# Two attention layers rebuilt on units of two tiles, with heads in row groups and the scores formed twice

## The chip, the cores and the metric

The kernel runs on one core of a Trainium2 chip. The metric is the device time of one execution in microseconds (us). Engines are named as in the profile: PE is TensorE (PEld its weight loads), DVE is VectorE, ACT is ScalarE, POOL is GpSimd, SP is SyncE, which here only issues DMAs.

## What is computed

The input is 128 sequences of 64 tokens of width 128, and a context of the same shape. Four stages follow one another; everything is fp32.

```python
x = x + _L0_xattn_ref(_layernorm(x), ctx, ctx, ...)   # 16 heads of 8, gate, three layer norms
x = x + _L0_ffn_ref(_layernorm(x), ...)               # 128 -> 512 -> 512 -> 512 -> 128
x = x + _L1_xattn_ref(_layernorm(x), ctx, ctx, ...)   # 16 heads of 8
x = x + _L1_ffn_ref(_layernorm(x), ...)               # 128 -> 512 -> 128
# both attentions, per sequence and head:
scores = jnp.einsum('bqhd,bkhd->bhqk', q, k) * scale
attn = jax.nn.softmax(scores, axis=-1)
out = jnp.einsum('bhqk,bkhd->bqhd', attn, v)
# layer 0 only: out = layer_norm(sigmoid(qn @ Wg) * (out @ Wo + bo))
```

The softmax takes the maximum of each row away before the exp.

## The kernel before

A tile is two sequences, 128 rows by 128 features; there are 64. The prologue (`prepare`, L170) loads and turns the weights and loads all of x and of the context into `x_res` and `ctx_res`. `attention` (L374) is called for layer 0 (`gated`) and layer 1, and each call is followed by a feed-forward stage on chunks of four tiles. Each of the four is a block of its own, which begins when all engines have left the one before. The feed-forward stages are not touched.

In `attention` every engine runs the same steps j over the tiles (`Steps`, L42: lead 5, lag 9, a loop unrolled by 4 in the middle, straight code at both ends), and in a step it works on several tiles, each at another place of its pipeline. The order on an engine is the order of the code, and semaphores tie the engines. For one tile:

- DVE takes the statistics (L733, L757), POOL the power -1/2 (`rstd`, L663), ACT normalises (`normed`, L617), PE turns it (`ps_in`, L517), ACT copies it (`turned`, L572), PE makes q, k and v in `ps_qkv` (L550, L551, L554), ACT copies them (L597, L600, L605).
- POOL spreads k over the heads: `k_heads` (L647) is k, repeated 16 times and multiplied by a mask that leaves each copy the 8 rows of its head, 2048 columns. PE then forms all 16 heads' scores with the full depth of 128 rows (L492): four fp32 products of 512 columns in two column halves, into the two banks `ps_s`.
- DVE takes the maximum of each row (`top`, L750) and subtracts it (`prob`, L776). Since `ps_s` exists once, the scores of the next tile wait for `shifted`. ACT takes the exp (L624), PE turns the result in eight pieces (`ps_pt`, L543), ACT copies it (`prob_t`, L591), and PE multiplies by the values (L533), two heads at a time, in four column groups. Two extra columns of ones in `v_by_pair` give the denominators.
- ACT copies (`sums_t`, L584), PE turns (L509), DVE divides (L694, L703), PE turns (L524), ACT copies (`out_t`, L579), PE multiplies by Wo (L502), and DVE adds the result to x (layer 1, L690) or goes through bias, gate and layer norm (layer 0, L686 to L743, where L714 multiplies `rstd` by the gate).

An fp32 product is two instruction pairs in the records (weight load and matmul each twice); a transposition is one.

Of the kernel before, what the change touches and what calls it, by code (L numbers as in the profile page):

```python
# [18 lines left out]
P = 128  # L19
# [7 lines left out]
UNROLL = 4  # L27

# [13 lines left out]
class Steps:  # L42
# [3 lines left out]
    def __init__(self, total, lead, lag, unroll):  # L46
        self.total, self.first, self.last, self.unroll = total, -lead, total + lag, unroll
        self.lo = -(-lag // unroll) * unroll
        self.hi = (total - lead) // unroll * unroll
# [120 lines left out]
def prepare(nc, t, a):  # L170


    with ExitStack() as ctx:
# [13 lines left out]
        cols = sb("cols", [P, 10])  # L187
        rows = sb("rows", [P, 3, P])
# [11 lines left out]
        zeros_ready, ident_ready, consts_ready = sem("zeros_ready"), sem("ident_ready"), sem("consts_ready")  # L200
        v_zero_ready = sem("v_zero_ready")
# [7 lines left out]
        with nc.Block() as block:  # L209
            @block.sync  # L210
            def _(sp):
                xv = a["x"].rearrange("(t b) s d -> (b s) t d", b=PER_TILE)
                cv = a["ctx_1024"].rearrange("(t b) s d -> (b s) t d", b=PER_TILE)
                xs = t.x[:, :].rearrange("p (t d) -> p t d", d=P)
                cs = t.ctx[:, :].rearrange("p (t d) -> p t d", d=P)

                def load_tiles(n):
                    first, last = (t.load_steps + [t.tiles])[n:n + 2]
                    sp.dma_start(xs[:, first:last, :], xv[:, first:last, :]).then_inc(t.tiles_loaded[n], 16)
                    sp.dma_start(cs[:, first:last, :], cv[:, first:last, :]).then_inc(t.tiles_loaded[n], 16)  # L220
# [18 lines left out]
            def _(act):  # L239
                names = ["L0_xattn_bq", "L0_xattn_bk", "L0_xattn_bv", "L0_xattn_ln_q_g", "L0_xattn_ln_q_b",  # L240
                         "L0_xattn_ln_kv_g", "L0_xattn_ln_kv_b", "L1_xattn_b_q", "L1_xattn_b_k", "L1_xattn_b_v"]
                for n, k in enumerate(names):
                    act.dma_start(cols[:, n:n + 1], column(a[k])).then_inc(params_loaded, 16)
                act.dma_start(rows[:, 0, :], row_everywhere(a["L0_xattn_Wg"].rearrange("d a -> (d a)"))).then_inc(params_loaded, 16)
                act.dma_start(rows[:, 1, :], row_everywhere(a["L0_xattn_ln_q_b"])).then_inc(params_loaded, 16)
                act.dma_start(rows[:, 2, :], row_everywhere(a["L0_xattn_ln_q_g"])).then_inc(params_loaded, 16)
# [16 lines left out]
            def _(pool):  # L263
                nc.gpsimd.memset(t.ident[:, :], 0.0).then_inc(zeros_ready, 1)
                nc.gpsimd.memset(t.head_mask[:, :], 1.0).then_inc(zeros_ready, 1)
                nc.gpsimd.memset(t.minus_half[:, :], -0.5)
                pool.wait_ge(zeros_ready, 2)
# [3 lines left out]
                nc.gpsimd.affine_select(out=t.head_mask[:, :], in_=t.head_mask[:, :], compare_op=ALU.is_ge, fill=0.0,  # L271
                                        base=0, pattern=[[-HEAD_DIM, HEADS]], channel_multiplier=1).then_inc(consts_ready, 1)
                pool.wait_ge(consts_ready, 1)
                nc.gpsimd.affine_select(out=t.head_mask[:, :], in_=t.head_mask[:, :], compare_op=ALU.is_ge, fill=0.0,
                                        base=HEAD_DIM - 1, pattern=[[HEAD_DIM, HEADS]], channel_multiplier=-1).then_inc(consts_ready, 1)
# [1008 lines left out]
```

## Time and profile before

| | |
|---|---|
| median of 3 runs | 1400.15 us (1397.81 to 1401.39) |
| span of the profiled execution | 1397.6 us |
| PE busy | 1187.9 us, 85% |
| DVE busy | 1097.0 us, 78% |
| ACT busy | 1015.8 us, 73% |
| POOL busy | 650.3 us, 47% |
| HBM read, written | 12.80 MB, 4.19 MB |

The span runs from the first to the last instruction of one execution; the runs are timed from outside. The shares are means over five stretches with different limits: the prologue (to about 48 us), attention 0 (to about 559), feed-forward 0 (to about 920), attention 1 (to about 1284) and feed-forward 1. Busy time says how long an engine held instructions, and an instruction that is held up counts as busy. So the stretches have to be read one by one, and in them the waits and the order in time.

### The profile page before, as it was taken

The page shows a single profiled execution, that of the slowest core. Times are in us where ns is not written, and L with a number is a line of the kernel's source. Part 1 is how long each engine was busy: PE and PEld are TensorE (multiplying, and loading weights), DVE is VectorE, ACT ScalarE, POOL GpSimd, SP SyncE. Part 2 cuts the span into 40 slices and gives each one's busy share as a digit, 9 for nine tenths or more (in the row PEclk, how much of TensorE's full clock was granted, in tenths as well). Part 3 has the DMA queues.
Part 4 walks back from the last instruction along what each step waited for, and adds up shares of the span by engine and source line. Part 5 has one row for each costly group of instructions (what it writes and reads, how often), then busy time and mean ns, then how long its engine had stood idle before and what let it go on. Part 6 is the DMA issues. An engine that isn't in the chain of part 4 may idle for free. (4 is left out here: it accounts for less than half of the span.)

```text
span 1397.6 us, 33684 instructions
## 1 busy us (share of the span) xinstructions
PE 1187.9 (85%) x10683; PEld 840.6 (60%) x10683; DVE 1097.0 (78%) x2885; ACT 1015.8 (73%) x2107; POOL 650.3 (47%) x449
## 2 busy tenths in 40 slices
PE   2686767777777775799999999969999999998998
PEld 2454544444444453688888888746666666665886
DVE  3599999999999997567667666437777777777996
ACT  2576566666666664688888888758888888885896
POOL 2766656566565663000000000058888888884110
PEclk8799999999999997899999999989999999999999
DMA  9400000000000000000000000000000000000011
GB/s 243 125 2 1 1 0 0 0 0 0 0 0 0 0 2 2 1 1 0 0 0 0 0 0 0 1 0 2 2 0 0 0 0 0 0 2 2 27 42 53
DMA packets 22080, 17.81 MB, mean 13 GB/s; under 512 B 2369, under 2 KB 17601, under 8 KB 22017
## 3 DMA queue, kind: packets, MB, share of 16 engines
q1 hardware_dynamic: 19792, 16.52, 4.1%
q0 software_dynamic: 352, 0.27, 0.2%
q8 instruction: 36, 0.59, 0.2%
q10 hardware_dynamic: 1872, 0.20, 0.1%
q14 instruction: 28, 0.22, 0.1%
HBM read 12.80 MB, written 4.19 MB: 12 GB/s over the span
## 5 line engine op out<-in xcount | busy, mean ns | idle before, releaser
L647 POOL TENSOR_TENSOR k_heads<-k_t,head_mask 128x2048 f32<-128x2048 f32 x128 | 462.6, 3614 | 57.5 <-ACT k_t L597 57.5
L492 PE MATMUL ps_s<-k_heads,q_t 128*64 128x512 f32 x1024 | 266.4, 640 | 134.7 <-DVE prob L776 133.7
L750 DVE TENSOR_REDUCE top<-ps_s 128x16 f32<-128x1024 f32 x128 | 155.8, 1217 | 111.0 <-PE ps_s L492 110.9
L663 POOL TENSOR_TENSOR rstd<-spread,minus_half 128x1 f32<-128x1 f32 (+2 forms) x140 | 95.0, 678 | 285.1 <-DVE spread L770 198.4
L126 POOL TENSOR_TENSOR front_rstd<-front_spread,minus_half 128x4 f32<-128x4 f32 x32 | 33.4, 1045 | 375.3 <-DVE front_spread L119 375.3
L799 PE MATMUL g_ps<-g_h_lo,w_hi 128*128 128x512 f32 x512 | 206.7, 404 | 0.0
L1015 DVE TENSOR_TENSOR g_h_lo<-g_h,g_h_hi 128x512 fp32r<-128x512 f32 x192 | 132.5, 690 | 92.3 <-ACT g_h_hi L963 88.4
L492 PEld LDWEIGHTS ps_s<-k_heads,q_t 128*64 128x64 f32 x1024 | 74.1, 139 | 217.2 <-issue 208.3
L800 PE MATMUL g_ps<-g_h_hi,w_hi 128*128 128x512 f32 x512 | 202.5, 395 | 0.0
L714 DVE TENSOR_TENSOR y_scale<-rstd,gate 128x1 f32<-128x1 f32 x64 | 171.0, 2671 | 0.1
L591 ACT ACTIVATE prob_t<-ps_pt 128x1024 f32<-128x1024 f32 x128 | 131.0, 1024 | 50.1 <-PE ps_pt L543 50.0
L776 DVE TENSOR_TENSOR prob<-ps_s,top 128x1024 f32<-128x1024 f32 x128 | 155.1, 1212 | 0.3
L624 ACT ACTIVATE prob<-prob 128x1024 f32<-128x1024 f32 x128 | 134.1, 1047 | 14.4 <-DVE prob L776 14.3
L543 PE MATMUL ps_pt<-ident,prob 128*128 128x128 f32 x1024 | 139.8, 280 | 0.2 <-ACT prob L624 0.2
L572 ACT ACTIVATE turned<-ps_in 128x256 f32<-128x256 f32 x128 | 49.1, 383 | 119.8 <-PE ps_in L517 118.2
L963 ACT ACTIVATE g_h_hi<-g_h 128x512 fp32r<-128x512 f32 x192 | 121.3, 632 | 18.7 <-DVE g_h L1025 14.6
L543 PEld LDWEIGHTS ps_pt<-ident,prob 128*128 128x128 f32 x1024 | 109.7, 141 | 12.1 <-ACT prob L624 0.6
L502 PEld LDWEIGHTS ps_y<-wa,out_t 128*128 128x128 f32 x256 | 41.8, 205 | 116.5 <-issue 112.4
L799 PEld LDWEIGHTS g_ps<-g_h_lo,w_hi 128*128 128x128 f32 x512 | 97.2, 190 | 22.6
L800 PEld LDWEIGHTS g_ps<-g_h_hi,w_hi 128*128 128x128 f32 x512 | 97.2, 190 | 21.0
L955 ACT ACTIVATE g_h<-g_ps,s 128x512 f32<-128x512 f32 x128 | 87.3, 682 | 30.4 <-PE g_ps L800 24.6
L533 PE MATMUL ps_o<-prob_t,v_by_pair 128*32 128x64 f32 x4096 | 85.5, 225 | 0.7 <-ACT prob_t L591 0.6
(171 smaller groups left out, 2503.2 us busy)
## 6 DMA issues: line engine op xcount, KB each, us to landing
out_x<-x_res SPq DMA_DIRECT2D x16, 256.0 KB, 2.3
raw_mid<-in_L_ffn_h_w SPq DMA_DIRECT2D x2, 1024.0 KB, 13.9
x_res<-in_x SPq DMA_DIRECT2D x2, 512.0 KB, 8.0
ctx_res<-in_ctx SPq DMA_DIRECT2D x2, 512.0 KB, 9.3
raw_up<-in_L_ffn_w_w SPq DMA_DIRECT2D x2, 256.0 KB, 7.7
raw_w<-in_L_ffn_W SPq DMA_DIRECT2D x2, 256.0 KB, 5.8
raw_down<-in_L_ffn_w_w SPq DMA_DIRECT2D x1, 256.0 KB, 14.6
raw_l<-in_L_xattn_Wq SPq DMA_DIRECT2D x1, 64.0 KB, 2.1
```

The source lines that it names most:

```text
L492: last = nc.tensor.matmul(ps_s[b * SEQ:(b + 1) * SEQ, half * 512:(half + 1) * 512], q_t[:, u, b * SEQ:(b + 1) * SEQ], k_heads[:, u % 2, ha ...
L543: last = nc.tensor.transpose(ps_pt[:, hp * P:(hp + 1) * P], prob[:, s % 2, hp * P:(hp + 1) * P], t.ident[:, :])
L591: nc.scalar.activation(prob_t[:, s % 2, :, :], ps_pt[:, :].rearrange("p (n d) -> p n d", n=PAIRS), ACT.Copy).then_inc(prob_t_taken, 1)
L624: nc.scalar.activation(prob[:, u % 2, :], prob[:, u % 2, :], ACT.Exp).then_inc(exp_done, 1)
L647: nc.gpsimd.tensor_tensor(k_heads[:, s % 2, :, :], k_t[:, s, :].unsqueeze(1).to_broadcast([P, HEADS, P]), t.head_mask[:, :].unsqueeze(2).t ...
L714: nc.vector.tensor_tensor(y_scale[:, 0:1], rstd[:, slot_a, 2:3], gate[:, slot_a:slot_a + 1], ALU.mult)
L750: nc.vector.tensor_reduce(out=top[:, u % 2, :], in_=ps_s[:, :].rearrange("p (h k) -> p h k", h=HEADS), op=ALU.max, axis=AX.X).then_inc(top ...
L776: nc.vector.tensor_tensor(prob[:, u % 2, :].rearrange("p (h k) -> p h k", h=HEADS), ps_s[:, :].rearrange("p (h k) -> p h k", h=HEADS), top ...
L799: nc.tensor.matmul(out, w_hi, x_lo, start=first and w_lo is None, stop=False)
L800: return nc.tensor.matmul(out, w_hi, x_hi, start=False, stop=last)
L963: nc.scalar.activation(h_hi[level][:, o, :], h[:, o % 2, :], ACT.Copy).then_inc(hi_ready[level], 1)
L1015: nc.vector.tensor_tensor(h_lo[level][:, o, :], h[:, o % 2, :], h_hi[level][:, o, :].bitcast(F32), ALU.subtract).then_inc(lo_ready[level], 1)
```

## The change

Both attentions are rewritten; the feed-forward stages stay. The steps now run over 32 units of two tiles, with lead 4 and lag 5.

- Wq, Wk and their biases are permuted on the host, so that the 32 rows of a group g hold 8 features of each of four heads. After the projection (now 256 columns wide, L580, L581) ACT copies to `qk_t`, and eight DMAs on SP's queue (L885) lay the heads side by side: `qk` has head set m at columns m*256, in rows 32g to 32g+7. Row 32g+8 of q takes minus the row maximum, and the same row of k holds ones.
- The scores of a tile are 32 small products, 8 rows deep, 64 by 64, in four row groups that write alternately to the two column halves (L488). DVE takes the maximum (L762). PE turns the maxima of a unit (L606), ACT copies them with the sign turned, four DMAs (L894) put them into `qk`.
- Two steps later PE forms the scores again with the operands exchanged and nine rows deep (L499): they come out transposed and with the maximum taken away, in `ps_st`. ACT takes the exp straight from there into `prob_t`.
- So `k_heads`, the subtraction, the eight transpositions and the copy of `prob_t` are gone.
- The context no longer lies in SBUF: a DMA per unit brings it (L870), in layer 1 from a transposed copy laid out on the host, so that layer 1 doesn't turn it. In layer 0 POOL normalises it (L735).
- The gate's product is formed on PE (L594), and the gate's power and the output norm's power are one power on POOL (L742) of two columns per unit. POOL also makes the small operands of the norms (L713 to L731).

The core of the diff:

```diff
+UNIT_TILES = 2
+UNIT = UNIT_TILES * P
+GROUPS = 4
+SETS = HEADS // GROUPS
...
     T = t.tiles
-    steps = Steps(T, lead=5, lag=9, unroll=UNROLL)
+    N = T // UNIT_TILES
+    steps = Steps(N, lead=4, lag=5, unroll=UNROLL)
...
+        qk = sb("qk", [P, UNROLL, 2, SETS, UNIT])
...
+        ps_st = psum("ps_st", 2)
+        ps_av = psum("ps_av")
+        ps_mid = psum("ps_mid")
+        ps_turn = psum("ps_turn")
+        ps_vy = psum("ps_vy")
...
+                def scores(i, s, k):
+                    for m in range(SETS):
+                        for b in range(PER_TILE):
+                            at = slice(k * P + b * SEQ, k * P + (b + 1) * SEQ)
+                            for g in range(GROUPS):
+                                rows, h2, bank = slice(32 * g, 32 * g + HEAD_DIM), g % 2, g // 2
+                                col = bank * 512 + (m * PER_TILE + b) * SEQ
+                                last = nc.tensor.matmul(ps_s[h2 * SEQ:(h2 + 1) * SEQ, col:col + SEQ],
+                                                        qk[rows, s, 0, m, at], qk[rows, s, 1, m, at], start=True, stop=True)
+                    last.then_inc(scores_done, 1)
+
+                def shifted_scores(i, s, k):
+                    for m in range(SETS):
+                        for b in range(PER_TILE):
+                            at = slice(k * P + b * SEQ, k * P + (b + 1) * SEQ)
+                            for g in range(GROUPS):
+                                rows, h2, bank = slice(32 * g, 32 * g + HEAD_DIM + 1), g % 2, g // 2
+                                col = bank * 512 + (m * PER_TILE + b) * SEQ
+                                last = nc.tensor.matmul(ps_st[h2 * SEQ:(h2 + 1) * SEQ, col:col + SEQ],
+                                                        qk[rows, s, 1, m, at], qk[rows, s, 0, m, at], start=True, stop=True)
+                    last.then_inc(shifted_done, 1)
+
+                def weighted_values(i, s, k):
+                    for b in range(PER_TILE):
+                        for half in range(2):
+                            for c in range(4):
+                                hp = 4 * half + c
+                                last = nc.tensor.matmul(
+                                    ps_av[PAIR_COLS * c:PAIR_COLS * (c + 1), (2 * k + half) * P + b * SEQ:(2 * k + half) * P + (b + 1) * SEQ],
+                                    t.v_by_pair[:, s, (k * PER_TILE + b) * PAIRS + hp, :],
+                                    prob_t[:, k, hp % 2, hp // 2, b, :], start=True, stop=True)
+                    last.then_inc(pv_done, 1)
...
+                def exponential(i, k):
+                    wait(act, shifted_done, 2 * i + k + 1)
+                    wait(act, pv_done, 2 * i + k - 1)
+                    nc.scalar.activation(prob_t[:, k, :, :, :, :].rearrange("p h m b q -> p (h m b q)"), ps_st[:, :],
+                                         ACT.Exp).then_inc(exp_done, 1)
...
+                        for n in range(2):
+                            last = nc.scalar.activation(qk_t[:, s % 2, n, :], ps_mid[:, n * UNIT:(n + 1) * UNIT], ACT.Identity,
+                                                        bias=t.qk_bias[:, layer, n:n + 1])
+                        last.then_inc(qk_taken, 1)
...
+                        wait(act, top_turned, i + 1)
+                        before = (u - 2) % UNROLL
+                        wait(act, top_landed[before], landed(i - 2, before, 4))
+                        nc.scalar.activation(minus_top_t[:, s % 2, :], ps_turn[0:32, 0:P], ACT.Copy, scale=-1.0).then_inc(top_taken, 1)
...
+                        wait(pool, pool_chain, 2 * i + 1)
+                        nc.gpsimd.tensor_tensor(rstd[:, s, :, :], spread[:, s, :, :],
+                                                t.minus_half[:, 0:NORMS * UNIT_TILES].rearrange("p (n k) -> p n k", n=NORMS),
+                                                ALU.pow).then_inc(pool_chain, 1)
...
+                            last = nc.gpsimd.tensor_scalar(normed[:, s % 2, 1, k, :], ctx_in[:, s, k, :], rstd[:, s, 1, k:k + 1],
+                                                           offset[:, s, 1, k:k + 1], ALU.mult, ALU.add)
+                        last.then_inc(ctx_normed, 1)
...
+                def maximum(i, s, k):
+                    wait(dve, scores_done, 2 * i + k + 1)
+                    wait(dve, top_turned, i - 1)
+                    nc.vector.tensor_reduce(out=top[:, s % 2, :, k, :], in_=ps_s[:, :].rearrange("p (a b q) -> p a b q", b=PER_TILE, q=SEQ),
+                                            op=ALU.max, axis=AX.X).then_inc(top_ready, 1)
...
+                        nc.vector.scalar_tensor_tensor(out=y_spread[:, s % 2, :], in0=gate_sq[:, span(i, UNIT_TILES)], scalar=EPS,
+                                                       in1=y_moments[:, s, :, 1], op0=ALU.mult, op1=ALU.add).then_inc(y_spread_ready, 1)
...
+                        wait(sp, qk_taken, i + 1)
+                        wait(sp, shifted_done, 2 * (i - 3))
+                        if isinstance(i, int) and i < UNROLL:
+                            wait(sp, ones_ready, i + 1)
+                        for g in range(GROUPS):
+                            for n in range(2):
+                                sp.dma_start(qk[32 * g:32 * g + HEAD_DIM, s, n, :, :],
+                                             qk_t[32 * g:32 * (g + 1), s % 2, n, :]).then_inc(qk_landed[s], 16)
...
+                        wait(sp, top_taken, i + 1)
+                        for bank in range(2):
+                            for h2 in range(2):
+                                row = 32 * (2 * bank + h2) + HEAD_DIM
+                                sp.dma_start(qk[row:row + 1, s, 0, :, :],
+                                             minus_top_t[16 * bank:16 * (bank + 1), s % 2, h2 * SEQ:(h2 + 1) * SEQ]).then_inc(top_landed[s], 16)
+                    load_ctx(ahead, slot)
```

Order on PE in attention 0 before, one tile step, just ahead of the loop. ps_in, ps_o and ps_pt are the banks for the turned inputs and sums, for the weighted values and for the turned probabilities.

```order
L492 MATMUL ps_s<-k_heads,q_t 64x512 x4
L502 MATMUL ps_y<-wa,out_t 128x128
L509 MATMUL ps_in<-ident,sums_t 128x128 x2
L517 MATMUL ps_in<-ident,normed 128x128 x2
L524 MATMUL ps_o<-ident,heads_out 128x128
L533 MATMUL ps_o<-prob_t,v_by_pair 32x64 x16
L543 MATMUL ps_pt<-ident,prob 128x128 x8
L550 MATMUL ps_qkv<-turned,wa 128x128
L551 MATMUL ps_qkv<-turned,wa 128x128
L554 MATMUL ps_qkv<-wa,turned 64x64 x4
```

The same place on PE now, one unit step, two tiles (ps_turn, ps_mid and ps_vy are the banks for turned inputs, for projections and turned sums, and for values and output).

```order
L488 MATMUL ps_s<-qk 64x64 x32
L499 MATMUL ps_st<-qk 64x64 x32
L533 MATMUL ps_turn<-ident,normed 128x128 x4
L543 MATMUL ps_mid<-ident,av 128x128 x4
L488 MATMUL ps_s<-qk 64x64 x32
L508 MATMUL ps_av<-prob_t,v_by_pair 32x64 x16
L559 MATMUL ps_turn<-ident,heads_out 128x128 x2
L499 MATMUL ps_st<-qk 64x64 x32
L570 MATMUL ps_vy<-wa,out_t 128x128 x2
L580 MATMUL ps_mid<-turned,wa 128x256
L581 MATMUL ps_mid<-turned,wa 128x256
L590 MATMUL ps_vy<-wa,turned 64x64 x8
```

It goes on with L594, L508 and L606. The eight transpositions per tile are gone, the small products have come in, and between any two blocks of scores there is other work.

SP's queue had nothing to do in attention before. It now has thirteen DMAs per unit; two units of layer 0:

```order
L870 DMA ctx_in<-in_ctx 128x2x128
L885 DMA qk<-qk_t 8x4x256 x8
L894 DMA qk<-minus_top_t 1x16x64 x4
L870 DMA ctx_in<-in_ctx 128x2x128
L885 DMA qk<-qk_t 8x4x256 x8
L894 DMA qk<-minus_top_t 1x16x64 x4
```

PE waits for the eight at the unit's first scores (two steps on) and for the four at its shifted scores.

## Rows read from the trace of the kernel before

**Rows 1.** Windows: busy us (instructions) of PE, PEld, DVE, ACT, POOL; granted clock; DMA share.

```profile
48.00:563.00 515.00, 379.50 (x4281) 241.56 (x4281) 495.07 (x1457) 321.18 (x766) 311.95 (x202) 0.91 0.01 2
927.00:1283.00 356.00, 339.41 (x4274) 223.08 (x4275) 258.02 (x568) 288.94 (x695) 291.10 (x189) 0.99 0.00 1
```

**Rows 2.** Line L750, the maximum, min/median/max ns, first and last start; whole, 500:560, 900:1000.

```profile
L750 DVE TENSOR_REDUCE top<-ps_s x128: 1203/1224/1227, 51.8 to 1272.1; 128x16 f32<-128x1024 f32 x128
...
L750 DVE TENSOR_REDUCE top<-ps_s x6: 1206/1208/1224, 501.1 to 535.5; 128x16 f32<-128x1024 f32 x6
...
L750 DVE TENSOR_REDUCE top<-ps_s x13: 1223/1225/1227, 932.7 to 995.8; 128x16 f32<-128x1024 f32 x13
```

**Rows 3.** Waits in 300:500 and in 1000:1200 (total us, times, longest).

```profile
PE ps_s L492 <- DVE prob L776: 52.6, 25, 2.6
...
DVE top L750 <- PE ps_s L492: 48.7, 37, 1.4
```

**Rows 4.** Groups by line and form: busy us, mean ns | idle before.

```profile
L647 POOL TENSOR_TENSOR k_heads<-k_t,head_mask 128x2048 f32<-128x2048 f32 x128 | 462.6, 3614 | 57.5 <-ACT k_t L597 57.5
...
L714 DVE TENSOR_TENSOR y_scale<-rstd,gate 128x1 f32<-128x1 f32 x64 | 171.0, 2671 | 0.1
...
L776 DVE TENSOR_TENSOR prob<-ps_s,top 128x1024 f32<-128x1024 f32 x128 | 155.1, 1212 | 0.3
```

**Rows 5.** Timeline of PE, one tile of attention 1: start us, us, work.

```profile
1124.73 1.94 PE L492 MATMUL ps_s<-k_heads,q_t 128*64 128x512 f32 x8 [0.39 <-DVE prob L776]
1126.59 0.49 PE L502 MATMUL ps_y<-wa,out_t 128*128 128x128 f32 x2
...
1127.14 0.38 PE L517 MATMUL ps_in<-ident,normed 128*128 128x128 f32 x2
...
1127.56 0.65 PE L533 MATMUL ps_o<-prob_t,v_by_pair 128*32 128x64 f32 x32
1128.14 1.09 PE L543 MATMUL ps_pt<-ident,prob 128*128 128x128 f32 x8
1129.07 0.39 PE L550 MATMUL ps_qkv<-turned,wa 128*128 128x128 f32 x2
1129.30 0.39 PE L551 MATMUL ps_qkv<-turned,wa 128*128 128x128 f32 x2
1129.61 0.45 PE L554 MATMUL ps_qkv<-wa,turned 128*64 128x64 f32 x8
1129.89 0.63 PE L492 MATMUL ps_s<-k_heads,q_t 128*64 128x512 f32 x2
```

**Rows 6.** Timeline of PEld, the weight loads of that block of L533.

```profile
1127.56 0.49 PEld L533 LDWEIGHTS ps_o<-prob_t,v_by_pair 128*32 128x32 f32 x32 [0.17 <-issue]
```

**Rows 7.** Groups by form that carry the loads of ACT, DVE and POOL.

```profile
L591 ACT ACTIVATE prob_t<-ps_pt 128x1024 f32<-128x1024 f32 x128 | 131.0, 1024 | 50.1 <-PE ps_pt L543 50.0
...
L572 ACT ACTIVATE turned<-ps_in 128x256 f32<-128x256 f32 x128 | 49.1, 383 | 119.8 <-PE ps_in L517 118.2
...
L617 ACT ACTIVATE normed<-x_res,offset,rstd 128x128 f32 x88 | 43.4, 493 | 4.4
...
L126 POOL TENSOR_TENSOR front_rstd<-front_spread,minus_half 128x4 f32<-128x4 f32 x32 | 33.4, 1045 | 375.3 <-DVE front_spread L119 375.3
...
L715 DVE SCALAR_TENSOR_TENSOR y_gain<-y,y_moments,ln_o_g 128x128 f32<-128x128 f32 x64 | 21.8, 341 | 0.1
...
L667 POOL TENSOR_TENSOR x_res<-x_res,ln_o_b 128x128 f32 x44 | 20.3, 462 | 0.0
```

**Rows 8.** SP's queue: lines L223 and L1212 (landing in us), and its timeline at 9 us.

```profile
L223 SPq DMA_DIRECT2D raw_l<-in_L_xattn_Wo x1: 431/431/431, 2.2 to 2.2; - x1
...
DMA to landing us min/median/max: 2.3/2.3/2.4
...
9.01 1.31 SPq L230 DMA_DIRECT2D raw_l<-in_L_xattn_w_k  x1
```

**Rows 9.** Page, DMA queues: packets, MB, share of 16 engines.

```profile
q8 instruction: 36, 0.59, 0.2%
```

More of the change, by code:

```diff
@@ L629, in step @@
-                    if gated and isinstance(j, int) and T + 4 <= j < T + 8:
-                        n = j - T - 4
+                        wait(act, offset_ready, i + 1)
+                        wait(act, in_t_done, i - 1)
+                        for k in range(UNIT_TILES):
+                            last = nc.scalar.activation(normed[:, s % 2, 0, k, :], t.x[:, span(i * UNIT_TILES + k, P)], ACT.Identity,
+                                                        scale=rstd[:, s, 0, k:k + 1], bias=offset[:, s, 0, k:k + 1])
@@ new lines, in step @@
+                        last.then_inc(x_normed, 1)
+                    i, s = j + 1, (u + 1) % UNROLL
+                    if gated and on(i):
+                        wait(act, v_taken, i + 1)
+                        nc.scalar.activation(gate_sq[:, span(i, UNIT_TILES)], gate_exp[:, span(i, UNIT_TILES)], ACT.Square,
+                                             bias=t.one[:, 0:1]).then_inc(gate_sq_ready, 1)
+                    if gated and isinstance(j, int) and N + 1 <= j < N + 5:
+                        n = j - N - 1
@@ L665, in step @@
[L665 to L668 removed]
+                        wait(pool, moments_ready, i + 1)
+                        wait(pool, x_normed, i - 3)
+                    if on(j):
+                        wait(pool, x_normed, j + 1)
+                        rows = t.x[:, span(j, UNIT)].rearrange("p (k d) -> p k d", d=P)
+                        nc.gpsimd.tensor_tensor(rows, rows, closing_row.unsqueeze(1).to_broadcast([P, UNIT_TILES, P]), ALU.add).then_inc(biased, 1)
@@ new lines, in step @@
+                    i, s = j - 3, (u - 3) % UNROLL
+                    if gated and on(i):
+                        wait(dve, y_taken, i + 1)
+                        wait(dve, y_chain, 2 * i)
+                        for k in range(UNIT_TILES):
+                            last = nc.vector.bn_stats(y_stats[:, s % 2, k, :], y[:, s, k, :])
+                        last.then_inc(y_chain, 1)
+                        wait(dve, y_chain, 2 * i + 1)
+                    i, s = j - 4, u
+                    if gated and on(i):
+                        wait(dve, y_gain_ready, i + 1)
+                        for k in range(UNIT_TILES):
+                            at = t.x[:, span(i * UNIT_TILES + k, P)]
+                            last = nc.vector.scalar_tensor_tensor(out=at, in0=y_gain[:, k, :], scalar=y_scale[:, s, k:k + 1], in1=at,
+                                                                  op0=ALU.mult, op1=ALU.add)
+                        last.then_inc(x_done, 1)
```

663 lines of the change are left out of this document (329 added, 334 removed).

## Prediction

> **What bounds the kernel now.** I first cut the span into its stretches and read busy time and clock in each [rows 1]; only the two attentions change. Then the spacing of one operation that occurs once a tile, the row maximum, gives the period [rows 2]: in attention 0 its 64 starts run from 51.8 to 535.5 us, 484/63 = 7.68 us a tile, in attention 1 from 932.7 to 1272.1, 339/63 = 5.39.
>
> In attention 0 DVE is busy for 495 of 515 us. Part of that is no work: the product `y_scale` of one column takes 2.67 us in the mean [rows 4]. It lies over POOL's spreading of k, 3.61 us each, and ends when that ends, so DVE is held up for some 2.5 us a tile. PE waits for DVE, for the subtraction that frees the scores' bank (52.6 us in 25 tiles [rows 3]).
>
> In attention 1 PE is busy for 339 of 356 us, 95%, at a clock of 0.99, and DVE waits for its scores (48.7 us in 37 tiles [rows 3]). PE and the ring scores, maximum, subtraction, next scores bind together. The bound there is what PE has to do in order, and after the change I expect it to be so in both attentions. So the sum is made on PE, from start to start in one tile [rows 5].
>
> **What goes.** Per tile on PE: the scores, 1124.73 to 1126.59 = 1.86 us, and the eight transpositions, 1128.14 to 1129.07 = 0.93, together 2.8 us (5.6 a unit). On DVE the subtraction, 1.21 us, and in attention 0 the hold-up with its cause; on POOL 3.6 us; on ACT one pass of 1.02 us.
>
> **What comes: S, the price of a block of scores.** A block is 32 products of 64 columns, 64 pairs of weight load and matmul, and a unit has four blocks, two of each form. No row shows products in different row groups, so I bound S.
> - Lower: the values' block also has small fp32 products of 64 columns, in four column groups. Its weight loads follow at (0.49-0.11)/31 = 12 ns [rows 6] (0.11 us is the length of one), its 32 pairs take 0.58 us from start to start with the change of shape [rows 5]. If four row groups run abreast as four column groups do, 64 pairs take 0.8 us and the change 0.2: S = 1.0.
> - Upper: if only the two column halves run abreast, the block streams just what the old scores streamed (64 x 64 columns against 8 x 512), 1.86 us. If nothing runs abreast, 3.7.
> - I take twice the values' block, S = 2 x 0.58 = 1.16: the nearest row in size, dtype and number abreast. It could not be below 0.93, a quarter of 3.7.
>
> **The rest of a unit on PE** [rows 5]. Values 2 x 0.58 = 1.16. Transpositions: three took 0.42 (1127.14 to 1127.56), 0.14 each; attention 1 has nine (input 2, sums 4, heads 2, maxima 1), 1.26. Two output products at 0.23 to 0.31, 0.54. q and k now have 256 columns: 0.31 + 0.23 for 128 columns each, twice that less one change, 0.95. v, 16 pairs against 8 in 0.28: 0.5. Sum 4.4, with 4S 9.05 us. Attention 0 has two transpositions more (0.28) and the gate's two products of one column (no dearer than 0.23 each, I take 0.3): 9.65. PE was busy for 95% where it bound before; by that share 9.5 and 10.2 us a unit, against 10.8 and 15.4 for two tiles now.
>
> **What lies beside it,** in us a unit. ACT: two exps at 1.02, three to four copies of 256 to 512 columns at 0.38 to 0.6, q, k and v 1.7, the norm 2 x 0.49, small ones: 6.4 in attention 1, 7.1 in attention 0 [rows 7]. DVE in attention 0: two maxima 2.44, twelve on 128 columns at up to 0.34 (4.1), small ones 0.6: about 7; in attention 1 about 4.3. POOL in attention 0: a power 1.05 and one of some 0.7, the bias 0.7, two norms at up to 0.46, five small ones: 4 to 5. DVE can still be held up by POOL, but now by operations of 1 us at most, once or twice: 8 to 9 of 10.2. No engine passes PE, and between a block of PE and the one that needs its product (scores to maximum, shifted scores to exp to values) lie 1.5 to 3 us of other PE work, more than the 1.02 to 1.22 that ACT or DVE takes. If that cover is gone, each unit pays up to the difference, 0.5 us, and this is what the 95% stand for.
>
> SP's queue: 13 DMAs at 0.43 us [rows 8] are 5.6 us of 9.5. Landing takes 2.3. A unit's eight heads' DMAs go out in the second half of its projection's step and are due a step later, the four of the maxima have a step too: 3.6 + 1.8 + 2.3 = 7.7 us, under a step of 9.5. Behind a waiting DMA stand the next context load (seven units ahead in layer 0, four in layer 1) and nothing else.
>
> **Ends.** Lead and lag were 14 tile steps and are 9 unit steps, and the first scores now need two hops by DMA and four memsets of `qk` on POOL. I add 10 us a layer, estimated as four tile steps' worth at a thin load. In the prologue half the initial load is gone, but x still comes first and the first context units queue behind it: nothing.
>
> **Sum.** Attention 0: 31 x 10.2 = 316 for 484, -168. Attention 1: 31 x 9.5 = 295 for 339, -45. Ends +20. 1397.6 - 193 = 1205 us of span; the median is 2.5 above the profiled span, so 1207.
>
> **Rivals.**
> 1. Two abreast. S = 1.86: the units' sums are 12.45 and 11.85, by 97% (other engines have more room) 12.8 and 12.2. Attention 0: 397, -87; attention 1: 378, +39; ends +20: 1372. For it: both row groups 0 and 1 write to one bank, 2 and 3 to the other, and v's products, two abreast, show no better than 27 to 35 ns a pair [rows 5]; weight loads of 64 columns may not go faster than this either. Against it: the loads of 32 columns come at 12 ns.
> The Trainium skill, TensorEngine Tiling (Array Packing), Gotcha 1: PSUM Pressure, says that different row tiles can't write to the same PSUM bank at the same time. By that rule this rival is what happens, unless the column halves count apart; no row here shows row tiles.
> 2. Slower: the row groups don't run abreast at all. S = 3.7, units of 19.9 and 19.2, attention 0 +133, attention 1 +256, ends +20: about 1807. The point from which the whole is slower: 31 times both units must pass 484 + 339 - 20 = 803, a mean of 13.0 a unit, S above 1.96 us or 31 ns a pair. Against it: column groups do run abreast.
> 3. Slower: SP's queue binds. At 9 us, with its queue full, an issue took 1.31 us instead of 0.43 [rows 8]; 13 of these are 17 us a unit, 1397.6 - 484 - 339 + 62 x 17 + 20 = 1650. It decides from 0.73 us an issue (9.5/13) on, and gives a loss from 1.0 on. Against it: that queue was full of megabytes, and here a unit moves some 0.4 MB (eight times 32 KB and 128 KB of context) in 9.5 us.
> 4. Instructions. A unit has 361 pairs, 722 instructions of PE in about 10 us, where a tile had 134. The instruction queue brought 0.59 MB in 36 packets [rows 9], 16 KB each, and a packet that takes 2.3 us as other DMAs do, one after the other, would carry a unit's 2.8 packets in 6.5 us; at twice that, 13 us a unit, as break-even: 1400.
> The Trainium skill, Runtime: NRT & Kernel Launch, Instruction fetch mechanics, gives PE room for 2048 instructions and says that a taken branch outside it waits for a fetch. The loop of four units has 2888, that of four tiles had 536. By this rule each of the 4 turns would pay once, an estimate of 2.3 us each, some 20 us in all.
>
> **Chances.** The forecast 0.62; two abreast 0.20; no row groups 0.06; SP's queue 0.05; instructions or another wait that takes half the gain 0.07. The range goes from 1140 (S = 0.93, little waiting: -0.92 x 62 = -57) to 1385, just past two abreast, and leaves out some 0.15. A measurement of this kernel can tell about 0.3%. Faster by more: 0.62 + 0.19 + 0.05 = 0.86; within: 0.02; slower: 0.12.
>
> **What the profile will show.** The spacing of L762 halves: two to a unit of 10.2 us and 9.5. The blocks L488 and L499: 1.16 us each from start to start in the forecast, 1.86 or 3.7 in the rivals; that is the first row to read. The one-column DVE hold-up of 2.67 us is gone. SPq L885 at 0.43. If PE has idle time ahead of L488 with the DMA of `qk` as releaser, SP is late; if its releaser is issue and the instruction queue shows several MB, it is the fetch. I am wrong at the root if S isn't near 1.16, and in the middle if S is right and the unit is still above 10.5 us.

## The result and the profile after

The changed kernel takes 1570.28 us (median of 4 runs, 1562.42 to 1579.78) against 1400.02 for the kernel before on the same chip: ratio 1.122, interval 1.119 to 1.125, slower by 12%. The prediction was 1207 us, faster. It missed by 363 us and on the wrong side.

The profiled execution has a span of 1561.3 us. Its windows (columns as in [rows 1]) over attention 0, the feed-forward behind it, attention 1, and two pieces of the attentions:

```profile
48.00:636.00 588.00, 546.04 (x11551) 459.05 (x11551) 227.28 (x721) 230.37 (x477) 125.26 (x269) 0.55 0.08 24
636.00:985.00 349.00, 335.56 (x1488) 267.56 (x1488) 218.76 (x464) 284.52 (x434) 22.54 (x33) 0.97 0.00 1
985.00:1445.00 460.00, 421.56 (x11279) 347.50 (x11276) 134.19 (x282) 185.46 (x377) 59.18 (x145) 0.66 0.11 31
...
100.00:150.00 50.00, 50.00 (x1044) 42.70 (x1039) 18.90 (x62) 19.33 (x41) 12.17 (x27) 0.50 0.09 25
1350.00:1400.00 50.00, 46.74 (x1429) 38.11 (x1430) 16.14 (x29) 23.29 (x51) 6.77 (x14) 0.81 0.13 37
```

PE is the bound, as forecast: busy 93% and 92% of the two attentions. DVE's 495 us of attention 0 [rows 1] are 227. What nobody had priced is the column behind POOL's. The granted clock is 0.55 and 0.66 where it was 0.91 and 0.99, and from 100 to 150 us it is 0.50, that is 1.2 GHz, with PE busy for all 50 us. Between the attentions it goes back to 0.97.

The maximum (line L762, answering to [rows 2]), first in attention 0 and then in attention 1:

```profile
L762 DVE TENSOR_REDUCE top<-ps_s x64: 1223/1224/1226, 58.0 to 569.7; 128x16 f32<-128x1024 f32 x64
...
L762 DVE TENSOR_REDUCE top<-ps_s x64: 1223/1225/1227, 990.3 to 1416.9; 128x16 f32<-128x1024 f32 x64
```

Two of them make a unit, so a unit takes 511.7/31.5 = 16.2 us and 426.6/31.5 = 13.5 us, where 10.2 and 9.5 were forecast.

The same program at its two clocks. PE's timeline (start us, us, work) at 402 us, in attention 0, and then a whole unit at 1353 us, in attention 1:

```profile
402.27 1.99 PE L499 MATMUL ps_st<-qk 9*64 9x64 f32 x64
404.19 1.22 PE L570 MATMUL ps_vy<-wa,out_t 128*128 128x128 f32 x4
...
409.04 1.08 PE L508 MATMUL ps_av<-prob_t,v_by_pair 128*32 128x64 f32 x32
410.05 0.40 PE L606 MATMUL ps_turn<-ident,top 128*32 128x128 f32 x1
410.38 1.99 PE L488 MATMUL ps_s<-qk 8*64 8x64 f32 x64
412.14 1.93 PE L499 MATMUL ps_st<-qk 9*64 9x64 f32 x64
414.00 1.11 PE L533 MATMUL ps_turn<-ident,normed 128*128 128x128 f32 x4
```

```profile
1353.31 1.16 PE L488 MATMUL ps_s<-qk 8*64 8x64 f32 x64
1354.29 1.11 PE L499 MATMUL ps_st<-qk 9*64 9x64 f32 x64
1355.34 0.44 PE L533 MATMUL ps_turn<-ident,normed 128*128 128x128 f32 x2
...
1356.14 1.16 PE L488 MATMUL ps_s<-qk 8*64 8x64 f32 x64
1357.23 0.97 PE L508 MATMUL ps_av<-prob_t,v_by_pair 128*32 128x64 f32 x32
...
1362.51 0.69 PE L488 MATMUL ps_s<-qk 8*64 8x64 f32 x32
```

From start to start a block of scores takes 1.76 to 1.92 us in the first and 0.98 to 1.09 in the second. The second unit runs from 1353.31 to 1362.51, 9.20 us, against my sum of 9.05 for it. So in units at full clock the working was right, and most units don't run at full clock. The question for the experiments is what takes the clock away from a PE that is busy, and what else stands between 9.2 us and a unit.

### The profile page after: what moved, and what is told of

Same layout as the page of the kernel before. It is cut to its first block and busy times, and to the rows that moved or that the text cites. A ratio compares the mean times of both kernels' runs of the same rounds, so it can differ in the third digit from the quotient of the medians.

```text
span 1561.3 us, 58912 instructions
## 1 busy us (share of the span) xinstructions
PE 1425.1 (91%) x24891; PEld 1172.7 (75%) x24891; DVE 694.7 (44%) x1829; ACT 803.8 (51%) x1467; POOL 241.6 (15%) x507
## 5 line engine op out<-in xcount | busy, mean ns | idle before, releaser
L762 DVE TENSOR_REDUCE top<-ps_s 128x16 f32<-128x1024 f32 x128 | 156.8, 1225 | 361.9 <-PE ps_s L488 272.7
L618 ACT ACTIVATE prob_t<-ps_st 128x1024 f32<-128x1024 f32 x128 | 131.0, 1024 | 228.8 <-PE ps_st L499 228.8
L499 PE MATMUL ps_st<-qk 9*64 9x64 f32 x8192 | 228.1, 284 | 21.7 <-issue 17.6
L488 PE MATMUL ps_s<-qk 8*64 8x64 f32 x8192 | 217.2, 278 | 31.3 <-issue 24.8
L488 PEld LDWEIGHTS ps_s<-qk 8*64 8x64 f32 x8192 | 194.9, 187 | 61.2 <-issue 49.6
L499 PEld LDWEIGHTS ps_st<-qk 9*64 9x64 f32 x8192 | 206.6, 193 | 45.4 <-issue 41.4
L508 PE MATMUL ps_av<-prob_t,v_by_pair 128*32 128x64 f32 x4096 | 126.3, 291 | 2.1 <-issue 1.7
L651 ACT ACTIVATE qk_t<-ps_mid,qk_bias 128x256 f32<-128x256 f32 x128 | 53.6, 470 | 118.8 <-PE ps_mid L581 118.8
L508 PEld LDWEIGHTS ps_av<-prob_t,v_by_pair 128*32 128x32 f32 x4096 | 97.4, 153 | 16.6 <-ACT prob_t L618 3.7
L570 PE MATMUL ps_vy<-wa,out_t 128*128 128x128 f32 x256 | 75.1, 446 | 0.9 <-ACT out_t L642 0.9
L533 PE MATMUL ps_turn<-ident,normed 128*128 128x128 f32 x192 | 50.1, 391 | 27.5 <-POOL normed L735 16.6
L580 PE MATMUL ps_mid<-turned,wa 128*128 128x256 f32 x128 | 67.5, 630 | 2.3 <-ACT turned L636 2.3
```

What stands on the lines that cost most here:

```text
L488: last = nc.tensor.matmul(ps_s[h2 * SEQ:(h2 + 1) * SEQ, col:col + SEQ], qk[rows, s, 0, m, at], qk[rows, s, 1, m, at], start=True, stop=True)
L499: last = nc.tensor.matmul(ps_st[h2 * SEQ:(h2 + 1) * SEQ, col:col + SEQ], qk[rows, s, 1, m, at], qk[rows, s, 0, m, at], start=True, stop=True)
L508: last = nc.tensor.matmul(ps_av[PAIR_COLS * c:PAIR_COLS * (c + 1), (2 * k + half) * P + b * SEQ:(2 * k + half) * P + (b + 1) * SEQ], t.v_b ...
L570: last = nc.tensor.matmul(ps_vy[:, k * P:(k + 1) * P], out_t[:, s % 2, k * P:(k + 1) * P], wo, start=True, stop=True)
L580: nc.tensor.matmul(ps_mid[:, 0:UNIT], wq, turned[:, s % 2, 0, :], start=True, stop=True)
L618: nc.scalar.activation(prob_t[:, k, :, :, :, :].rearrange("p h m b q -> p (h m b q)"), ps_st[:, :], ACT.Exp).then_inc(exp_done, 1)
```

## Experiments

All share one base: each is compared with the kernel before on its own chip. "Few rows" means that a head's 8 dimensions (9 with the maximum) fill 8 or 9 of the 32 rows of a row group.

**PE alone, in streams.** No attention, one program of PE that forms products one after the other from data in SBUF; half of x is copied out and nothing else is computed. Between the streams stand 16 products of 128 rows and 512 columns (14.0 us at full clock in the trace).

```
for k in range(512):    # L59: 8 rows of a row group, four groups abreast
    matmul(bank[o, c], wide[r:r + 8, ...], wide[r:r + 8, ...])
for k in range(512):    # L63: 32 rows, the first 8 hold the same numbers as in L59, the other 24 zeros
    matmul(bank[o, c], thin[r:r + 32, ...], thin[r:r + 32, ...])
...                     # L67: 32 rows, data in all; L71: 128 rows, 64 columns; L80: 8 rows, 512 columns
```

> This kernel computes nothing of the reference: it copies the first half of x to both halves of the output and lets PE alone run six streams of fp32 products, each behind a stretch of sixteen full products (128 rows, 128 columns of weights, 512 columns, 13.6 us at half the full clock) that should bring the clock up. The streams: 512 products of 8 rows in four row groups; the same with 32 rows a group, of which 8 hold data and the rest zeros; the same with 32 rows of data; 256 products of 128 rows in two column halves; 512 of 128 rows in four column groups of 32; 64 of 8 rows and 512 columns. The theory (T1): the clock follows how much of the array works, not whether PE is busy. Then the 8-row stream falls to a granted clock of 0.5 behind the dense stretch and its blocks of 64 pairs take 1.8 us instead of 0.95, while the streams of 128 rows stay at 1.0. T1 leaves open whether 32 rows help. Rival (T2): the clock falls because PE waits for DMAs and instructions, and a stream without waits stays at 1.0 with 8 rows too: 512 products in 15.2 us instead of 27. Rival (T3): small products of any depth do it; then the 128-row streams of 64 columns fall too.

PE's timeline of the 8-row stream and of the stream of 32 rows with 24 of them zero, and windows: around the first stream, over the second, and in the streams of L71 and L80:

```profile
32.00 3.02 PE L59 MATMUL bank<-data 8*64 8x64 f32 x191
36.00 2.61 PE L59 MATMUL bank<-data 8*64 8x64 f32 x128 [0.98 <-issue]
39.45 19.89 PE L59 MATMUL bank<-data 8*64 8x64 f32 x705 [0.84 <-issue]
...
83.09 2.09 PE L63 MATMUL bank<-thin 32*64 32x64 f32 x128 [1.64 <-issue]
86.55 2.09 PE L63 MATMUL bank<-thin 32*64 32x64 f32 x128 [1.36 <-issue]
90.00 2.09 PE L63 MATMUL bank<-thin 32*64 32x64 f32 x128 [1.36 <-issue]
```

```profile
32.00:36.00 4.00, 3.02 (x192) 2.88 (x192) 0.00 (x0) 0.00 (x0) 1.00 0.02 4
36.00:40.00 4.00, 3.16 (x148) 2.97 (x152) 0.00 (x0) 0.00 (x0) 0.67 0.02 4
40.00:56.00 16.00, 15.96 (x596) 15.77 (x592) 0.00 (x0) 0.00 (x0) 0.50 0.02 5
64.00:120.00 56.00, 46.32 (x1338) 30.31 (x1337) 0.00 (x0) 0.00 (x0) 0.99 0.01 3
...
160.00:164.00 4.00, 4.00 (x146) 4.00 (x142) 0.00 (x0) 0.00 (x0) 1.00 0.01 4
...
236.00:240.00 4.00, 4.00 (x24) 1.33 (x20) 0.00 (x0) 0.00 (x0) 0.50 0.00 0
```

On 8 rows PE is hardly ever idle, and the clock goes from 1.00 to 0.50 behind it; 705 pairs then take 19.89 us, 1.8 us for 64. On 32 rows, with the same numbers and 24 rows of zeros a group, it stays at 1.00 (0.99 over the whole window), although PE pauses more. So idle time doesn't make the clock fall here (T2). Nor does the size of the products (T3): on 128 rows, 64 columns each and PE busy for 4.00 of 4 us (160 to 164 us), the clock is 1.00, and on 8 rows, 512 columns each and PE as busy (236 to 240 us), it is 0.50. What the falling streams share is the few rows; that the added rows hold zeros doesn't matter.

The streams also show a second thing. At full clock the matmuls come 128 at a time in 2.09 us, and then PE stands still on issue for 1.36 to 1.64 us. 128 pairs are 256 instructions. This program has no loop, 4960 pairs of PE, and its instruction queue brings 0.64 MB in 39 packets of 16 KB: that makes 64 B an instruction, so such a burst is one packet. In the timeline one packet comes in 3.45 to 3.73 us, and the DMA records of the queue have them 3.3 to 3.8 us apart in both streams. So 512 products take 27.3 us on 8 rows (32.00 to 59.27) and 26.4 on 32 (75.86 to 102.23): both get their instructions at the same pace, and what the clock costs has to be read from the kernel.

**All 32 rows.** Rows 8 to 31 of each group are set (0 in q's half, 1 in k's) and go into both products.

```diff
-rows = slice(32 * g, 32 * g + HEAD_DIM)        # L486, and HEAD_DIM + 1 in L497
+rows = slice(32 * g, 32 * g + 32)
+nc.gpsimd.memset(qk[:, s, 0, :, :], 0.0)
```

> The scores' products take all 32 rows of their group instead of 8 or 9; the other rows hold zeros in q and ones in k, so the added terms are nothing. PE's instructions and their columns are the same. T1, if rows that carry zeros count as work: the granted clock of the attentions rises from 0.55 and 0.66 towards 1.0 and the time falls to 1200 to 1300 us. T1, if the chip looks at what the rows do and zeros are nothing: 1570 as the changed kernel, clock as it was. T2 (waits bring the clock down): 1570, no change either. T3 (small products as such): 1570.

Measured 1343.1 us, ratio 0.958 (0.955 to 0.961): 227 us of the loss were this, and the change is now a gain, though a smaller one than the 1200 to 1300 that T1 had. The windows of the attentions:

```profile
48.00:420.00 372.00, 318.83 (x10685) 268.61 (x10685) 193.55 (x610) 191.65 (x425) 120.92 (x265) 0.94 0.13 38
...
790.00:1226.00 436.00, 348.30 (x11418) 287.67 (x11416) 151.22 (x321) 205.82 (x417) 71.54 (x169) 0.93 0.12 34
```

The columns multiplied, the instructions and the transfers are the same; the clock is 0.94 and 0.93.

The expectation says that the added terms are nothing, and that isn't so for all. Row 8 of a group is set to 0 only once, ahead of the units, and then holds minus the maxima of the unit that had the same quarter of `qk` four units earlier. From the fifth unit on the first form adds them, so what is taken for the maximum, and taken away, is the maximum less that older number. A shift of a whole row doesn't change its softmax, so the same is computed, but what is taken away is no longer the row's own maximum. This holds for every 32-row kernel below, and no run here tries inputs with large scores.

A unit still takes 12.0 us in the middle of attention 0 (52 maxima from 99.2 to 405.5 us), not 10.2. PE's timeline at 192 us, the first matmuls after a turn of the loop:

```profile
191.96 1.57 PE L488 MATMUL ps_s<-qk 32*64 32x64 f32 x64 [3.53 <-issue]
193.28 0.31 PE L499 MATMUL ps_st<-qk 32*64 32x64 f32 x1
195.22 1.98 PE L499 MATMUL ps_st<-qk 32*64 32x64 f32 x63 [1.63 <-issue]
197.13 1.11 PE L533 MATMUL ps_turn<-ident,normed 128*128 128x128 f32 x4
```

Six such pauses of 3.22 to 3.85 us stand in the trace, three to an attention, four units apart. The expectation of the loop experiment below says five a loop; it is four turns with three jumps back. The pause shown has a second one behind it, and the clock falls for some microseconds too (1.98 for a block). So a long pause costs clock on 32 rows too.

**More dense work instead.** The changed kernel, with one product of 128 rows and 512 columns of fp32r ahead of each block of scores, into the bank that the block then overwrites.

```diff
+nc.tensor.matmul(ps_s[:, 0:512], t.w_hi[:, 0, 0:P], t.w_hi[:, 1, :], start=True, stop=True)
```

> Ahead of each of the four blocks of scores in a unit PE does one product more than it needs, 128 rows, 128 columns of weights and 512 columns in fp32r, into the bank that the block then overwrites: 0.23 us each at full clock, 0.92 us a unit, 62 unit periods. By the work alone (T2, T3) the kernel gets slower by 57 us at full clock and by up to 110 at half: 1630 to 1680. T1: the added work raises the granted clock, and the unit falls from 16.8 us towards 10.1: 1250 to 1500 us, with the clock of attention 0 above 0.7.

Two runs gave 1452.2 and 1495.1 us, the profiled one a span of 1493.3, with a clock of 0.73 and 0.79 in the attentions. PE does 256 products more, and the kernel is faster by 75 us or more. That fits the reading of the streams and no reading in which PE has simply too much to do. A clock of 0.73 is also only half way back.

**Only the first form on 32 rows.**

```diff
-rows = slice(32 * g, 32 * g + 32)              # in the second form only
+rows = slice(32 * g, 32 * g + HEAD_DIM + 1)
```

> The changed kernel with the products of the first form (for the maximum) on all 32 rows of a row group, and those of the second form left on 9 rows. Theory that few rows in use let the granted clock fall however busy PE is: the 9-row blocks alone are a third of PE's stream in a unit, so the clock should be between the changed kernel's (0.55 and 0.66 in the two attentions) and the 32-row kernel's (0.94 and 0.93), and the time between 1343 and 1570, near 1430. Rival, that the zeroed rows cured something else than the clock (reads of rows beside the heads): whichever form it sits in, the clock in the attentions would be all or nothing, 1343 or 1570 within 15 us.

1379.5 us, ratio 0.985 (0.979 to 0.992), clock 0.89 and 0.83. It lies between the two, as the theory had it and its rival (all or nothing) hadn't, but much nearer to 32 rows than my 1430: one form of the two brings back 191 of the 227 us. The loss is not in proportion to the number of blocks on few rows; why, no run shows. The windows of the attentions:

```profile
48.00:440.00 392.00, 343.69 (x11035) 289.55 (x11033) 198.31 (x620) 196.13 (x434) 121.33 (x264) 0.89 0.12 36
820.00:1260.00 440.00, 363.99 (x11338) 300.20 (x11337) 141.14 (x306) 192.25 (x394) 71.35 (x169) 0.83 0.11 34
```

**The loops written out.** On the 32-row kernel, each engine's steps stand one behind the other in the attentions.

```diff
     def run(self, eng, step):
+        if self.unroll == UNROLL:
+            for j in range(self.first, self.last):
+                step(j, j % self.unroll)
+            return
```

> The kernel with products on all 32 rows of a row group (1343.1 us), and attention's loops written out instead of turned: every unit's instructions stand one behind the other on all engines, so no engine jumps back. Nothing else differs. Theory that the turns of the loop cost PE time (in the trace of the 32-row kernel PE stands still for about 3.5 us on nothing but issue at a turn, 5 turns in each attention): 1305 to 1325 us. Theory that what is missing is PE's instruction supply at any place (256 instructions in a run and then a pause of 1.4 to 1.9 us, as in the streams alone): the turns go, the pauses inside the units stay, so the gain is at most these 35 us and units stay near 11 us. Rival, that SP's queue of transfers (9.3 us a unit in that trace) sets the pace and the pauses at the turns are only where it shows: within 5 us of 1343.

1304.2 us, ratio 0.934 (0.931 to 0.936). The long pauses are gone and 39 us with them, more than the some 21 us that the six pauses add up to. In the two attentions PE's waits on issue fall from 101 to 72 us, and the clock between the first maximum and the last rises from 0.95 in both to 0.97 and 0.98. A unit is 11.35 us in the middle of attention 0 (52 maxima from 99.6 to 389.0), and PE's longest waits between 100 and 360 us (total, times, longest) are all of one kind:

```profile
PE ps_st L503 <- issue: 14.3, 16, 1.7
PE ps_av L512 <- issue: 3.1, 4, 1.0
PE ps_s L492 <- issue: 2.8, 7, 0.8
```

The packets of the instruction queue are 3.9 us apart here (the median in each attention), and a unit needs 2.8 of them: 10.9 us.

**The same edit on 8 rows.** The edit above, on the changed kernel.

> The changed kernel (products on 8 and 9 rows) with attention's loops written out. If the clock is what costs it its time, PE at 0.50 asks for instructions at half the pace, and neither the loop's turns nor the supply hold it: 1540 to 1575 us, a smaller gain than the 39 us which the same edit gave at full clock, and a granted clock still near 0.55 and 0.66. Rival, that the loop's turns (pauses of PE) let the clock fall: with them gone the clock would be over 0.9 and the time near 1304.

1521.4 us (ratio 1.087, 1.077 to 1.096), 49 us less, which is more than I expected. A turn's pause is as long at the low clock (3.1 to 3.8 us in the changed kernel, 21 us in all), and PE's waits on issue in the two attentions fall by 29 us; the other 20 are not accounted for. The clock stays at 0.53 and 0.66. So the loop's pauses are not what makes it fall, and that rival is out.

**The same edit on the kernel before.**

> The kernel before, with attention's loops written out in the same way. It issues a third of the matmuls a tile (its scores are 4 matmuls of 512 columns a tile), waits on VectorE's prob 133.7 us in all and shows no pause on issue in its attentions: I expect 1390 to 1402 us, so that the 1304 us of the 32-row kernel without loops are the rewrite's and not the unrolling's. Rival: turns of the loop cost it as much as the rewritten kernel, 1360 to 1370 us.

1393.5 us, ratio 0.994 (0.993 to 0.996). The kernel before loses 7 us to its loops, not 39: the gain of the kernel above is the rewrite's.

**The maxima's transfers on POOL's queue** (on the 32-row kernel with loops written out).

```diff
-sp.dma_start(qk[row:row + 1, s, 0, :, :], minus_top_t[...])
+nc.gpsimd.dma_start(qk[row:row + 1, s, 0, :, :], minus_top_t[...])
```

> The written-out kernel of the row above, and the four transfers that lay the maxima into their rows issued on POOL's queue rather than SP's. It takes 4 x 0.72 = 2.9 us a unit from SP's queue (9.3 to 6.4 us). Theory that SP's queue still binds in a part of the units: 20 to 40 us under the written-out kernel, units near 10.2. Theory that PE's instructions bind: within 8 us of the written-out kernel. Against both: POOL's issue of a transfer may be so much slower than SP's that the maxima land later and PE waits on them ahead of the shifted scores: slower by 10 us or more.

1304.4 us against 1304.2: nothing. PE waits for transfers of `qk` for 6.7 us in the whole run, in four waits. SP's issues took 8.8 and 11.2 us in two units of the written-out kernel (near 220 us) and 6.4 in one of this, and they didn't bind.

**The keys' transfers on ACT's queue, besides.**

```diff
-for n in range(2): sp.dma_start(qk[...n...], qk_t[...n...])
+sp.dma_start(qk[...0...], qk_t[...0...])        # q on SP
+nc.scalar.dma_start(qk[...1...], qk_t[...1...]) # k, behind ACT's own copy
```

> The kernel of the row above, and the four transfers that lay the keys into their row groups issued on ACT's queue, so that SP has five transfers a unit (3.6 us), ACT and POOL four each. ACT's own queue is lengthened by four issues a unit (4 x 0.72 = 2.9 us beside some 6.3 us of work in a unit). If PE's instructions bind: within 8 us of the written-out kernel. If landing of keys and queries binds: 10 to 30 us faster than the kernel with the maxima on POOL. If ACT's issues hold up the exponentials: 10 us or more slower.

1445.5 us, ratio 1.033 (1.031 to 1.035). ACT's timeline at 201 us shows why, and under it the longest of PE's waits:

```profile
201.17 3.19 ACTq L663 DMA_DIRECT2D qk<-qk_t  x4
204.46 0.77 ACT L673 ACTIVATE v_by_pair<-ps_vy 64x256 f32<-64x256 f32 x2 [3.32 <-issue]
```

```profile
PE ps_turn L537 <- ACT normed L690: 128.4, 63, 10.7
```

Four issues hold ACT up for 3.19 to 3.94 us a unit. All that it does behind them comes later, and PE waits two us a unit for the norm. The clock falls besides, to 0.87 and 0.88 between the first maximum and the last of each attention, where it was 0.97 and 0.98, and PE is busy for 98 us more with the same work. So a wait in every unit costs clock on 32 rows too.

**Half the instructions for the same columns.** On the 32-row kernel with loops written out: one product of 128 columns in place of two of 64. The second sequence of a tile gets scores made with the first one's heads, so what is computed differs there; columns and all other work stay.

```diff
-for b in range(PER_TILE):
+for b in range(1):    # lhsT: sequence 0; rhs: both sequences
-    matmul(ps_s[..., col:col + SEQ], qk[rows, s, 0, m, at], qk[rows, s, 1, m, at])
+    matmul(ps_s[..., col:col + P],   qk[rows, s, 0, m, at], qk[rows, s, 1, m, wide])
```

> The written-out 32-row kernel (1304.2 us) with half as many score products, each of twice the columns: one product of 128 columns takes the place of the two of 64 of a head's two sequences, with the first sequence's heads as its weights for both. The second sequence's scores are therefore the wrong ones (they are formed from the first's queries or keys); PSUM is filled as before and all other work is unchanged. PE multiplies as many columns; its matmuls a unit fall from 355 to 227. Theory that the supply of instructions holds PE in that kernel (355 matmuls at 128 in some 3.6 us are 10.0 us, and its units take 11.0): the pauses on issue go, a unit takes the sum of PE's own work, 9.0 to 9.6 us, and the time is 1304 - 64 x 1.5 = 1210, range 1200 to 1230 us. Rival, that its units are held by the chain through ACT, DVE and the landing of transfers, and the pauses called issue are filled otherwise: 1295 to 1305 us.

1212.9 us, ratio 0.867 (0.864 to 0.869). The maxima of both attentions, and PE's timeline:

```profile
L767 DVE TENSOR_REDUCE top<-ps_s x64: 1223/1224/1226, 58.9 to 356.2; 128x16 f32<-128x1024 f32 x64
...
L767 DVE TENSOR_REDUCE top<-ps_s x64: 1223/1225/1226, 772.3 to 1074.7; 128x16 f32<-128x1024 f32 x64
```

```profile
221.10 1.10 PE L492 MATMUL ps_s<-qk 32*64 32x128 f32 x32
...
230.51 1.10 PE L492 MATMUL ps_s<-qk 32*64 32x128 f32 x32
```

A block's 32 pairs take the time of its 64 before, the unit is 9.4 us (221.10 to 230.51), and in PE's waits between 100 and 360 us no line with issue is left (the longest sum is 3.3 us, on the transfer of the maxima). PE's columns cost what they cost; 91 us had been the arrival of its instructions (PE's waits on issue in the two attentions of the written-out kernel were 72).

In attention 1 another limit appears: PE waits 25.2 us, in 18 waits, for the transfers of the maxima. SP issues there without a break, 9.1 us in the unit from 915.13 to 924.77 and 10.1 in the one before, for units of 9.6. So SP's queue, which didn't bind as long as instructions held PE, is full at this pace. No run here takes transfers off it in this kernel.

## Why the prediction was wrong

The way from the measurement to the forecast, each step one experiment: 1570 changed; 1343 with 32 rows (the clock, 227); 1304 without loops (39); 1213 with the scores' instructions halved (91). The forecast was 1207. The last kernel is near the one I had priced, one whose PE runs at full clock and never wants for instructions, but it issues half of the scores' instructions, which my sum didn't ask for, and forms wrong scores for every second sequence. That it lands within 6 us of the forecast is in part luck: against the kernel before, its attentions gain 224 us where I had 213, and its ends cost 36 where I had 20.

- **The step that failed: durations at a constant clock.** Every term of PE came from rows at a clock of 0.99 [rows 1, 5], and I carried them over as if the clock belonged to the chip and not to the work. The four blocks of scores of a unit turned a stream on all 128 rows (k's spread heads against all of q) into one on 32 or 36 rows. No row of before shows such a stream, so the clock was an unknown that should have had its two bounds: 9.65 us a unit at one end, twice that at the other. Twice is 19.3 and 18.1 us: 31 x 37.4 - 484 - 339 + 20 = +356, a span of 1754, and a range that reaches across 1400. Even a chance of 0.3 for it would have changed the range.
- **S**, the price I thought would decide, was near: 1.16 forecast, 0.98 to 1.09 measured at full clock, half of what two abreast would take. Four row groups do run abreast. Rivals 1 and 2 (1.86, 3.7) are out, and the 1.86 that I named as their sign did show up in the trace, 1.76 to 1.92 in attention 0. Only the clock beside it tells that it is another cause: the values' block of L508, which the rivals leave alone, takes 1.01 us (409.04 to 410.05) for 0.58 [rows 5] as well.
- **Trainium skill, TensorEngine Tiling (Array Packing), Gotcha 1: PSUM Pressure.** It excludes that different row tiles write to one PSUM bank at the same time. Groups 0 and 1 write to one bank, in different partitions, and 64 pairs took 1.0 us, not 1.86 or 3.7. Here the measurement decides: this arrangement ran abreast.
- **The unit's sum**, 9.05 forecast and 9.20 measured, is right by two errors that cancel. The four blocks of scores take 4.2 us (0.98, 1.05, 1.09, 1.09) for 4.6, and the rest 5.0 for 4.4.
- **The share of 95%** was too high even at full clock. I took it from a kernel with some third of the instructions. At full clock with 8192 + 8192 + 4096 small pairs, PE was busy for 86% (318.83 of 372) in the 32-row kernel.
- **Rival 4, instructions**, had a chance of 0.07 and was treated as an alternative to the forecast, when it is a term of it. 2.8 packets a unit at the 3.45 to 3.73 us that the streams show are 9.7 to 10.4 us: above PE's own 9.2, whatever else goes well. I had put a packet at 2.3 us. (A unit of attention 0 is 359 pairs in the trace, not 361, and 353 in attention 1.) In attention 0 of the changed kernel the low clock hid it, since a unit of 16.2 us wants less. The Trainium skill, Runtime: NRT & Kernel Launch, Instruction fetch mechanics, has a taken branch outside the held instructions wait for a fetch. The runs agree: 3.1 to 3.9 us of pause at a jump back, gone when written out. I had estimated 2.3 a turn and 20 us in all; the six pauses are 21 us, and writing the loops out gave 39 and 49.
- **SP's queue**: 0.43 us an issue was the wrong row. The lines of the changed kernel (min/median/max ns):

```profile
L885 SPq DMA_DIRECT2D qk<-qk_t x512: 657/672/1918, 49.0 to 1405.5; - x171
...
L894 SPq DMA_DIRECT2D qk<-minus_top_t x256: 502/589/1804, 69.9 to 1425.6; - x128
```

  Thirteen are 8.3 us a unit at the medians, not 5.6, close to the 9.5 from which I said it decides. It didn't bind in this kernel: PE waits 3.6 us on the transfers of L885 in the whole run. Nor did it bind in the written-out one, where moving the maxima's four changed nothing. At the pace that I had forecast it would have: see the last experiment, attention 1.
- **Ends**: first maximum 6 us later, the stretch from the last of attention 0 to the first of attention 1 420.6 us for 397.2, the end 144.4 for 125.5: 49 us where I had 20.
- **DVE's hold-up** went (DVE's operation of two columns ahead of the power, L846, takes 0.16 us, where `y_scale` took 2.67), and the gain that hung on it is real: in the last experiment attention 0 takes 297 us from its first maximum to its last, for 484, and attention 1 302 for 339; -187 and -37, where I had -168 and -45.

What stays open: why few rows in use bring the clock down at all, why one form on 32 rows gives back 84% of the loss, and why the stretch of attention 1 keeps more of its clock (0.66) than attention 0 (0.55). No run here takes these apart, and none has between 9 and 32 rows to a group.

## What to carry to other kernels

Before pricing a matmul stream by rows of another kernel, ask how many of the array's rows it uses: this kernel was turned from a 12% loss into a 4% gain by letting its products run over all 32 rows of a group, the added ones holding zeros against ones. Then count instructions beside columns, since a stream of short fp32 products can be held by their arrival (here 128 pairs in some 3.6 us), and a loop body of some 2900 PE instructions paid 3.1 to 3.9 us at each jump back, where one of 536 shows no such pause. The best kernel that still computes all of it is the 32-row one with its attention loops written out, 1304 us, 6.7% under the kernel before. Its row of maxima would have to be set back to zero for each unit if the number taken away is to be the row's own maximum; no run has that.

## What the hardware showed that was not expected

- TensorE's granted clock fell from 1.00 to 0.50 (2.4 to 1.2 GHz) under a PE that was busy for 15.96 of 16 us, on products of 8 rows of a group, and stayed at 0.99 to 1.00 on products of 32 rows, 24 of them zeros, in a window where it was busy for 46.32 of 56 us.
- At full clock the small products come in bursts of 128 matmuls with pauses of 1.4 to 1.6 us on issue; at half clock such a stream runs without a pause and takes about as long (27.3 us for 512 products, 26.4 at full clock).
- Issuing a transfer between partitions of SBUF took 0.67 us on SP for 32 KB and 0.8 to 1.0 on ACT, which does nothing else meanwhile; for 4 KB it took 0.59 on SP and 0.52 on POOL.
